# Largest value spread by one matmul, three rounding sums on GpSimd, and idle matmuls in an attention and fp8 feed-forward kernel

## What is computed

```python
x = x + attn(cond(x, weights1, itok), wq, wk, wv, wo)   # 32 heads, 8 key/value heads, causal
h = cond2(x, itok, weights2)                            # 32x32 mix of the tokens by condition
amax = max(abs(h)); s = max(amax, 1e-12) / 448          # over the whole tensor
q = fp8_e4m3(clip(h / s, -448, 448))
f = (q * s) @ (fp8_e4m3(qweight) * weight_scale).T + bias
fmax = max(abs(f)); fs = max(fmax, 1e-12) / 448         # over the whole tensor
x = x + clip(f / fs, -448, 448) * fs
```

## Time and profile before

| | us |
|---|---|
| median of 3 runs | 550.75 (550.38 to 551.4) |
| the profiled execution, its own time | 550.2 |
| its span | 548.4 |
| PE busy | 519.4 (95%) |
| DVE busy | 353.9 (65%) |
| ACT busy | 212.3 (39%) |
| POOL busy | 232.1 (42%) |
| mean granted TensorE clock, share of full speed | 0.974 |

### The profile page before, as it was taken

One profiled execution on the slowest core, in us unless ns is written; L12 is line 12 of the kernel. 1 busy time (PEld: TensorE's weight loads), 2 busy tenths in 40 slices (PEclk: granted clock), 3 DMA queues, 4 the chain that ended last, 5 costly groups with the idle time before them and its releaser, 6 DMA issues.

```text
span 548.4 us, 8842 instructions
## 1 busy us (share of the span) xinstructions
PE 519.4 (95%) x3244; PEld 414.9 (76%) x3244; DVE 353.9 (65%) x536; ACT 212.3 (39%) x372; POOL 232.1 (42%) x184
## 2 busy tenths in 40 slices
PE   4999999999999999999999999999999999999680
PEld 2987888888888888888888888888888888887420
DVE  5538255666676667666766676667566756675697
ACT  2514214342534263416341634253516251612524
POOL 4426422642664266426632673267326732610002
PEclk9899999999999999999999999999999999999875
DMA  7540500020012011201020202020202000000004
GB/s 250 178 154 0 173 2 1 1 97 1 16 64 96 0 32 44 96 0 52 24 96 0 73 3 96 0 76 2 93 0 76 5 1 0 2 1 0 2 0 153
DMA packets 18046, 26.88 MB, mean 49 GB/s; under 512 B 1995, under 2 KB 6219, under 8 KB 18028
## 3 DMA queue, kind: packets, MB, share of 16 engines
q1 hardware_dynamic: 18028, 26.63, 14.4%
HBM read 24.53 MB, written 2.10 MB: 49 GB/s over the span
## 4 chain that ended last, share of the span: by engine, by line
PE 90%; DVE 7%; issue 1%; DMA 1%; SPq 0%; ACT 0%; DVEq 0%
PE bank L526 27%; PE bank L527 26%; PE bank L528 26%; PE bank L590 3%; PE bank L577 3%; PE bank L518 1%; PE bank L645 1%; DVE f_max L911 1%; PE bank L506 1%; DVE xacc L964 1%; DVE v_all L959 1%; DMA wsc<-in_L_ffn_weight_scale 1%; DVE w L759 1%; DVE q_cos L212 1%; DVE v_all L906 0%
## 5 line engine op out<-in xcount | busy, mean ns | idle before, releaser
L780 DVE TENSOR_TENSOR q_cos<-bank,cst 128x512 f32<-128x512 f32 x80 | 55.3, 691 | 105.1 <-ACT q_swap L396 105.1
L295 POOL TENSOR_TENSOR q_rot<-q_cos,q_swap 128x512 f32<-128x512 f32 x64 | 82.6, 1291 | 89.1 <-DVE q_swap L782 89.1
L526 PE MATMUL bank<-wo_hi,o_hi 128*128 128x512 f32 x256 | 101.6, 397 | 1.2 <-issue 1.2
L526 PE MATMUL bank<-hT_hi,wq_hi 128*128 128x512 f32 x256 | 101.3, 396 | 0.0
L527 PE MATMUL bank<-wo_lo,o_hi 128*128 128x512 f32 x256 | 99.8, 390 | 0.0
L527 PE MATMUL bank<-hT_lo,wq_hi 128*128 128x512 f32 x256 | 99.8, 390 | 0.0
L528 PE MATMUL bank<-wo_hi,o_lo 128*128 128x512 f32 x256 | 99.6, 389 | 0.0
L528 PE MATMUL bank<-hT_hi,wq_lo 128*128 128x512 f32 x256 | 99.6, 389 | 0.0
L395 ACT ACTIVATE q_swap<-bank 64x512 f32<-64x512 f32 x80 | 47.7, 596 | 132.1 <-PE bank L528 132.1
L825 DVE TENSOR_TENSOR xacc<-xacc,bank 128x512 f32<-128x512 f32 x64 | 43.4, 677 | 42.7 <-PE bank L528 42.5
L274 POOL TENSOR_TENSOR wo_lo<-raw_o,wo_hi 128x512 fp32r<-128x512 f32 x32 | 43.7, 1387 | 58.7 <-ACT wo_hi L385 58.7
(11 more groups left out here) (137 smaller groups left out, 721.5 us busy)
## 6 DMA issues: line engine op xcount, KB each, us to landing
raw_q<-in_L_attn_wq SPq DMA_DIRECT2D x8, 1024.0 KB, 5.6
raw_o<-in_L_attn_wo SPq DMA_DIRECT2D x8, 1024.0 KB, 5.2
xacc<-in_x SPq DMA_DIRECT2D x4, 512.0 KB, 8.0
raw_k<-in_L_attn_wk SPq DMA_DIRECT2D x8, 256.0 KB, 2.7
out<-xacc SPq DMA_DIRECT2D x8, 256.0 KB, 2.0
raw_o<-in_L_attn_wv SPq DMA_DIRECT2D x1, 1024.0 KB, 6.8
raw_q<-in_L_attn_wv SPq DMA_DIRECT2D x1, 1024.0 KB, 6.8
q_rot<-in_L_ffn_qweight SPq DMA_DIRECT2D x1, 1024.0 KB
```

The costliest lines, as they stand in the source:

```text
L295: pool.tensor_tensor(dst, q_cos[b][:], q_swap[b][:], ALU.add).then_inc(rope_done, 1)
L526: pe.matmul(dst, l_hi, r_hi, start=(i == 0), stop=False)
L780: dve.tensor_tensor(by_t(q_cos[b][:]), by_t(q_ps[ITEM_BANK[k]][:]), cos_b, ALU.mult).then_inc(rope_cos, 1)
```

## The change

Four edits:

1. The spreading is one matmul: the column, repeated 128 times as the stationary operand, by the identity. This puts all 128 values in every partition, and VectorE's second reduction then works on 128 partitions and writes `col`. The row of ones leaves the constants.
2. The sums of tiles 2, 4 and 6 are made by GpSimd, as two instructions (`max` in place, then an add into `s_exp`). These tiles' `y_exp` already holds the maximum when VectorE rounds it.
3. `magic` runs two tiles ahead of the rounding, not one.
4. `hold_clock` puts matmuls whose result is not used (on `w8`, into bank 2) on TensorE: 3 ahead of the first spreading matmul and 16 behind it.

```diff
+SUM_POOL = (2, 4, 6)
...
-        y_sum = [flat(p_tr), flat(s_nat)]
+        y_sum = lambda t: flat(s_exp) if t in SUM_POOL else flat((p_tr, s_nat)[(t + 1) // 2 % 2])
...
+            for i, t in enumerate(SUM_POOL):
+                pool.wait_ge(y8_magic, t + 1)
+                pool.tensor_scalar(y_exp(t), y_exp(t), LEAST, None, ALU.max).then_inc(y8_least, 1)
+                pool.wait_ge(y_div_done, t + 1)
+                pool.wait_ge(y8_least, i + 1)
+                if i > 0:
+                    pool.wait_ge(y8_done, SUM_POOL[i - 1] + 1)
+                pool.tensor_tensor(y_sum(t), y_exp(t), y_div(t), ALU.add).then_inc(y8_sum_pool, 1)
...
-                pe.transpose(ps[0:1, 0:P], col[:, 4 * n:4 * n + 1], ident).then_inc(tail_mm, 1)
-                pe.wait_ge(tail_vec, 5 * n + 2)
-                pe.matmul(ps[:, P:P + 1], cst[0:1, C_ONE:C_ONE + P], row[0:1, n:n + 1],
+                pe.matmul(ps[:, 0:P], col[:, 4 * n:4 * n + 1].broadcast_to([P, P]), ident,
                           start=True, stop=True).then_inc(tail_mm, 1)
 
+            def hold_clock(count):
+
+                for _ in range(count):
+                    pe.matmul(bank[2][:], w8[:, 0, 0:P], w8[:, 0, :], start=True, stop=True)
+
+            hold_clock(3)
             spread_max(0)
+            hold_clock(16)
...
-                dve.wait_ge(tail_mm, 2 * n + 1)
-                dve.tensor_reduce(row[0:1, n:n + 1], ps[0:1, 0:P], AX_X, ALU.max).then_inc(tail_vec, 1)
-                dve.wait_ge(tail_mm, 2 * n + 2)
-                return ps[:, P:P + 1]
+                dve.wait_ge(tail_mm, n + 1)
+                dve.tensor_reduce(col[:, 4 * n:4 * n + 1], ps[:, 0:P], AX_X, ALU.max).then_inc(tail_vec, 1)
+                dve.wait_ge(tail_vec, 5 * n + 2)
+                return col[:, 4 * n:4 * n + 1]
...
-                dve.wait_ge(y_div_done, t + 1)
-                dve.wait_ge(y8_magic, t + 1)
-                dve.scalar_tensor_tensor(out=y_sum[t % 2], in0=y_exp(t), scalar=LEAST, in1=y_div(t), op0=ALU.max,
-                                         op1=ALU.add).then_inc(y8_sum, 1)
+                if t not in SUM_POOL:
+                    dve.wait_ge(y_div_done, t + 1)
+                    dve.wait_ge(y8_magic, t + 1)
+                    dve.scalar_tensor_tensor(out=y_sum(t), in0=y_exp(t), scalar=LEAST, in1=y_div(t), op0=ALU.max,
+                                             op1=ALU.add).then_inc(y8_sum, 1)
...
-                elif t < TILES - 1:
-                    magic(t + 1)
-                dve.wait_ge(y8_sum, t + 1)
...
+                elif t < TILES - 2:
+                    magic(t + 2)
+                if t in SUM_POOL:
+                    dve.wait_ge(y8_sum_pool, SUM_POOL.index(t) + 1)
+                else:
+                    dve.wait_ge(y8_sum, t + 1 - sum(p < t for p in SUM_POOL))
...
                     magic(1)
+                    magic(2)
                     dve.wait_ge(bias_hi_done, 1)
```

More of the change, by code:

```diff
@@ L35 @@
 LEAST = 1.5 * 2.0 ** 14
-C_COS, C_SIN, C_SVAL, C_CSEL, C_BLOCK, C_IDENT, C_TRI, C_ONE = 0, 32, 64, 68, 100, 104, 232, 264
-C_WIDTH = C_ONE + P
+C_COS, C_SIN, C_SVAL, C_CSEL, C_BLOCK, C_IDENT, C_TRI = 0, 32, 64, 68, 100, 104, 232
+C_WIDTH = C_TRI + T
 V_LATE = 4
 BY_POOL = (1, 3)
+SUM_POOL = (2, 4, 6)
 BIAS_ROWS = 33
@@ L70, in constant_table @@
     table[:, C_TRI:C_TRI + T] = np.where(np.arange(T)[None, :] > part[:, None] % T, MASKED, 0.0)
-    table[0, C_ONE:C_ONE + P] = 1.0
     return table
@@ L123, in build @@
         col = sb("col", [P, 12])
-        row = sb("row", [1, 4])
         ones_r = sb("ones_r", [BIAS_ROWS, P], F32R)
@@ L154, in build @@
         y_mm, y_copied, y_amax, tail_mm, tail_vec = (sem(n) for n in ("y_mm", "y_copied", "y_amax", "tail_mm", "tail_vec"))
-        y_div_done, y_exp_done, y8_magic, y8_sum, y8_done = (
-            sem(n) for n in ("y_div_done", "y_exp_done", "y8_magic", "y8_sum", "y8_done"))
+        y_div_done, y_exp_done, y8_magic, y8_sum, y8_sum_pool, y8_least, y8_done = (
+            sem(n) for n in ("y_div_done", "y_exp_done", "y8_magic", "y8_sum", "y8_sum_pool", "y8_least", "y8_done"))
         bias_step, bias_done, bias_hi_done = (sem(n) for n in ("bias_step", "bias_done", "bias_hi_done"))
@@ L931, in _ @@
                     dve.tensor_scalar(bias_sc, bias_row, col[0:BIAS_ROWS, 10:11], None, ALU.mult).then_inc(bias_done, 1)
-                elif t < TILES - 1:
-                    magic(t + 1)
-                dve.wait_ge(y8_sum, t + 1)
-                dve.scalar_tensor_tensor(out=y8[:, t, :], in0=y_exp(t), scalar=LEAST, in1=y_sum[t % 2], op0=ALU.max,
+                elif t < TILES - 2:
[4 more added lines that the diff above has]
+                    dve.wait_ge(y8_sum, t + 1 - sum(p < t for p in SUM_POOL))
+                dve.scalar_tensor_tensor(out=y8[:, t, :], in0=y_exp(t), scalar=LEAST, in1=y_sum(t), op0=ALU.max,
                                          op1=ALU.subtract).then_inc(y8_done, 1)
```

## The result

The kernel after takes 554.51 us, median of 12 runs (552.0 to 556.93); the kernel before took 550.45 us beside it (12 runs, 549.84 to 551.48). The ratio is 1.0073, with a 95% interval of 1.0061 to 1.0085: slower by 4.1 us, or 0.7%. The profiled execution of after took 554.79 us, its span is 553.0, against 550.2 and 548.4 before: 4.6 us more.

The account below looks back on a forecast made before the run. VectorE's own instructions and what blocks them were taken to bound the stretch after attention. The terms -0.5 - 0.1 + 0 + 1.0 - 1.8 + 3.9 gave +2.5 us on 550.75, so 553.3 us, range 551.6 to 555.8.

Parts of the forecast that it names:

- rival 3: Feed-forward tiles: a dear GpSimd max (554.9 us), a slow TensorE clock at the end (554.2), or both (555.8); chance 0.20.
- What bounds the stretch: From 514.3 to 534.1 us, only VectorE's own instructions and what blocks them cost time; it never waits for TensorE.
- Spreading, -0.5: Largest value over partitions, twice: one matmul replaces transpose, one-row reduction and matmul pair, gaining 0.25 us each.
- Constants, -0.1: Program start: the table loses 128 of 392 columns, so the wsc load behind it lands slightly earlier, 0.1 us gained.
- Idle matmuls, 0: Around the first spreading: nineteen unused matmuls cost nothing and bring nothing, since VectorE doesn't wait for the tiles.
- Rival 3's clock: Last feed-forward tile: TensorE at half clock makes the last maximum wait 0.85 us longer, 554.2 us; within a 0.20 chance.
- Magic(2), +1.0: Early feed-forward tiles: VectorE stands idle before magic(2) until ScalarE ends y_exp(2), costing 1.0 us (0.9 to 1.1).
- Three sums, -1.8: Feed-forward tiles 2, 4 and 6: their sums leave VectorE, saving 3 x 0.60 us.
- GpSimd's blocking, +3.9: Feed-forward tiles: GpSimd's max and add make VectorE's SBUF instructions wait, 3.9 us in all with 0.2 for handing over.
- GpSimd's max, taken at 0.6 us: Sums of tiles 2, 4, 6: the one-input max, shown in no row, priced near the 0.61 us copy, at most 1.29.
- Rivals 1 and 2: Offload: first, GpSimd hides beside VectorE, 549.35 us, chance 0.10; second, only two-input instructions collide, 552.2, chance 0.17.
- Rival 3's dear max: Feed-forward sums: GpSimd's max takes 1.29 us, making the change +4.1 us, 554.9 us; within a 0.20 chance.

Follow-up runs that it names:

- before_narrow: The kernel before with only the constants' table narrowed to 264 columns, the row of ones coming from a memset; 550.44 us, ratio 1.0002.
- after_again: The repetition: the changed kernel run once more, unchanged; 552.53 us against 550.43, ratio 1.0042.
- after_wide: The changed kernel with the old constants' table width of 392 columns; 552.97 us, ratio 1.0055.
- after_wsc_late: The changed kernel with the load of wsc moved behind the first loads, on its own semaphore, awaited only at first use; 551.77 us, ratio 1.0026.
- the probe: Two probes on the kernel before: eight unused GpSimd one-input maxima, or eight unused two-input adds, beside the feed-forward tiles; 555.92 and 556.28 us.
- no_pool_wide: The changed kernel with the 392-column table and all eight sums on VectorE, none on GpSimd; 550.66 us, ratio 1.0006.
- spread_only: The kernel before with the single-matmul spreading alone, table width kept; 549.57 us, ratio 0.9984.
- magic2_late_wide: The changed kernel with the 392-column table and magic(2) moved behind the bias' low part and sum(1); 552.88 us, ratio 1.0043.
- spread_hold: The kernel before with the single-matmul spreading and the 19 idle matmuls; 549.59 us, ratio 0.9997.

## Why the prediction was right, and where its steps were not

The direction was right, and the time, 554.51 against 553.3 forecast, lies inside the stated range. It lies above the forecast's own range of 552.5 to 554.2, where rival 3 stood; the repetition has 552.53. Against before that is +4.1 and +2.1 us where +2.5 was forecast. The part that can be compared best is the stretch from R1 to R2: the prediction's terms for it (one spreading -0.25, +1.0, -1.8, +3.9) give +2.85, measured +2.96 and +2.94. By its steps:

- **What bounds the stretch** (VectorE's own instructions and what blocks them): right. The 2.96 us are made up of VectorE rows that lengthened, vanished or waited. "VectorE never waits for TensorE there" is true of the two profiles compared, but of few others.
- **Spreading, -0.5:** some 0.2 for each of the two, so -0.4. VectorE's next instruction came 0.85 us behind the matmul's start, where 0.75 was said.
- **Constants, -0.1:** a gain is not shown; before_narrow tells no difference (1.0002), and wsc lands no earlier with the smaller table. The step took the landing of wsc as given, and here the forecast missed the first measurement: the profiled execution has +1.85 us at R1. It is not an effect of the change (after_again), and the bounds 0 and 1.0 of gain had no room for it.
- **Idle matmuls, 0:** no gain, as said, in both directions of the test, and they were over 0.23 us before tile 0. Rival 3's clock came true in part: the half clock at the last tile, forecast at 0.85, cost 1.17 in after_wide, 1.72 in after_wsc_late and nothing in after and after_again. It is not tied to the change, since before_narrow waits there too.
- **Magic(2), +1.0:** 0.93 of idle time. Right.
- **Three sums, -1.8:** right.
- **GpSimd's blocking, +3.9:** 3.93 in the rows, and two tiles take 4.83 us (rounding to rounding, 525.17 to 530.00) where 4.8 was said, but the pieces were others. The walk had three magics (3, 5, 7) wait 1.1 each; in fact the roundings of tiles 1, 3 and 5 did, and the three magics hardly (0.27, 0.08, 0.09). The reason is the step behind it, **GpSimd's max, taken at 0.6 us with bounds 0.61 and 1.29: it took 1.97 and 1.86.** With a longer max the add starts one VectorE instruction later, beside the rounding. The text said that a max over 0.8 us would prove it wrong, and by that test this step was wrong. The sum survived, since a second error went against it: a one-input max does not hold VectorE off for its length; the three together cost 0.74. Had they blocked in full, the loss would have been larger (the prediction's own price for a max of 1.29 was 1.7 more). The right total is partly luck.
- **Rivals 1 and 2** are out by their mechanism: the six instructions block VectorE for 3.9 us, and magic, with one input, is lengthened beside a max and beside an add (0.69 and 1.26 instead of 0.42). The second figure is the probe's, for in the changed kernel only roundings, with two inputs, ended up beside an add; and rival 2's time of 552.2 is nearer to the repetition's 552.53 than the forecast's 553.3. no_pool_wide shows the sign: without the offload the change costs nothing that can be told, with it 2 us.
- **Rival 3's dear max** came, and dearer than its 1.29, but not its price: the stretch is +2.96, not 1.7 above the forecast. That the first median lies in rival 3's range is owed to what is ahead of R1, as far as its profile shows.

On the port the Trainium skill, "SBUF — State Buffer", "SBUF: two separate sides", says that whichever instruction starts first has the pair of ports for its whole length and the other blocks. The add agrees with it (rounding over 0.55 us behind the add's end, twice). The one-input max doesn't: sum(1) began and ended inside it, and sum(3) did so without losing anything.

Two slips of the recorded text: a max at 1.29 us gives +4.2 by its own 1.7, not +4.1, and the 3.45 us of wsc are not in rows 8, though the trace has them. It also leans on numbers without a row. These are rows of the kernel before for them (VectorE beside GpSimd, VectorE alone, the matmuls at the slow clock, and the first spreading's pair):

```profile
49.17 1.66 DVE L756 SCALAR_TENSOR_TENSOR p_tr<-s_exp,q_rot 128x512 f32<-128x512 f32 x1
...
40.59 0.69 DVE L759 SCALAR_TENSOR_TENSOR w<-s_nat,p_tr 128x512 bf16<-128x512 f32 x1
...
520.60 1.89 PE L705 MATMUL bank<-q_cos,q_rot 128*128 128x512 bf16 x4
...
513.90 0.38 PE L687 MATMUL bank<-row,cst 1*128 1x1 f32 x2 [0.37 <-DVE row L888]
```

**Open:** what the median of spread_only gained beyond its 0.41 us; at what point of a one-input max VectorE is held, since some instructions lose 0.4 us beside it and others nothing; what decides whether the last tiles meet the slow clock, and how often; what wsc's landing time hangs on; and what makes the stretch between the first cast and 45 us 37.7 to 39.2 us long. A lead of three tiles, or an add on ScalarE, was not tried.

## What to carry to other kernels

Before work is moved from VectorE to GpSimd, look for a stretch of the trace in which the two already run side by side on SBUF, and charge the lengthened instructions of that stretch: here 1.8 us of work taken off cost 3.9 us of blocking. Count the instructions that the other engine needs for what was one fused instruction, and treat the price of one that no row shows as open upward, not between two kinds that look alike. A change at the end of a kernel should be read between two points of its own stretch, because a 0.5 KB load that the first instruction waits for, and need not, can move a single execution by 2 us.

## What was not expected of the hardware

- GpSimd's `tensor_scalar` max of 128x512 fp32 with one SBUF input took 1.85 to 1.97 us in the changed kernel and 1.48 at best (magic2_late_wide; 1.49 in the probe), where the two-input add took 1.10 to 1.53. The Trainium skill, "GPSIMD Engine Reference", "Elementwise — side-by-side cycle accounting", has 769 ns for 512 elements in its best loop; no max here comes near.
- That max lengthens a VectorE instruction on SBUF by 0.41 us at most, whatever its own length, and some not at all; the shorter add by up to 1.07.
- One load of 0.5 KB at the start landed between 3.0 and 3.8 us after its issue in eleven profiles, and at 6.2 in one, with the same four loads ahead of it as in the repetition, where it took 3.8.
- Idle matmuls that kept TensorE at 2.4 GHz to 524.4 us, instead of 516.7, were followed by a slow stretch to 531.3 in after and spread_hold, and by none in no_pool_wide.
